# Attention output by way of DRAM, twenty output projections in the last attention stage, smaller loads of x and other idle products

## The reference

```python
x = x + 0.5 * ffn(layernorm(x))    # router over 8 experts, one chosen, gate = its probability
x = x + attn(layernorm(x))         # 16 heads of 8 features, rope, causal softmax, @ Wo.T
x = x + 0.5 * ffn(layernorm(x))    # the same weights again

# ffn, on t tokens
idx = argmax(softmax(xt @ Wr + br)); gates = max(...)
xn = layernorm(xt) * ln_g + ln_b
h = relu(xn @ W1[idx] + b1[idx]);  y = (h @ W2[idx] + b2[idx]) * gates
# attn
score = q @ k.T, masked above the diagonal
out = softmax(score / sqrt(8)) @ v;  return out @ Wo.T
```

## Time and profile before

| | us |
|---|---|
| median of three runs | 799.37 (796.62 to 800.66) |
| profiled execution | 801.17 |
| its span, first to last instruction | 799.4 |
| TensorE busy | 760.2 (95%), 5441 instructions |
| VectorE busy | 609.4 (76%) |
| ScalarE busy | 506.5 (63%) |
| GpSimd busy | 313.7 (39%) |
| mean granted clock of TensorE, share of full | 0.975 |

### The profile page before, as it was taken

One profiled execution on the slowest core, in us unless ns is written; L12 is line 12 of the kernel. 1 busy time (PEld: TensorE's weight loads), 2 busy tenths in 40 slices (PEclk: granted clock), 3 DMA queues, 4 the chain that ended last, 5 costly groups with the idle time before them and its releaser, 6 DMA issues. The chain is left out here.

```text
span 799.4 us, 17413 instructions
## 1 busy us (share of the span) xinstructions
PE 760.2 (95%) x5441; PEld 427.2 (53%) x5441; DVE 609.4 (76%) x1919; ACT 506.5 (63%) x1229; POOL 313.7 (39%) x603
## 2 busy tenths in 40 slices
PE   9989999898999999999999999999999988999994
PEld 6669897555433344333434444443344337578894
DVE  5557775489998988898889888988988706856663
ACT  2146663376357787778778777877787782066662
POOL 6067754156522234223322332242234220077753
PEclk8799999999999999999999999999999998999998
DMA  9712211227550332033113312330330001222210
GB/s 283 290 46 53 54 43 46 96 55 194 150 90 18 54 62 47 16 61 61 35 29 60 62 24 39 63 54 15 55 62 3 1 2 36 111 53 52 52 38 27
DMA packets 27990, 51.85 MB, mean 65 GB/s; under 512 B 7552, under 2 KB 19200, under 8 KB 26496
## 3 DMA queue, kind: packets, MB, share of 16 engines
q1 hardware_dynamic: 21296, 41.04, 22.0%
q0 software_dynamic: 4096, 8.69, 4.1%
q10 hardware_dynamic: 2512, 1.06, 0.5%
HBM read 35.40 MB, written 14.97 MB: 63 GB/s over the span
## 5 line engine op out<-in xcount | busy, mean ns | idle before, releaser
L1424 DVE CUSTOM_DVE_ANT_0 cst<-psS,mask_row 128x768 bf16<-128x768 f32 (+7 forms) x512 | 361.9, 755 | 41.8 <-PE psS L1297 37.8
L1387 ACT ACTIVATE prob<-psST 128x512 f32<-128x512 f32 (+3 forms) x750 | 320.2, 498 | 108.2 <-PE psST L1329 87.2
L1344 PE MATMUL a_psO<-prob,vs 128*32 128x512 f32 (+3 forms) x1536 | 157.5, 496 | 0.4 <-ACT p_anT L1393 0.2
L1495 POOL TENSOR_TENSOR a_gate<-a_zeros 1x1 f32<-1x1 f32 x128 | 23.4, 183 | 290.9 <-ACT prob L1387 290.7
L1329 PE MATMUL psST<-a_qs,ks 75*128 75x512 bf16 (+1 forms) x480 | 125.8, 328 | 0.0
L1297 PE MATMUL psS<-ks,a_qs 72*128 72x512 bf16 (+2 forms) x480 | 112.4, 326 | 0.1
L790 POOL DMA_INDIRECT tok<-rows,f_there_number x64 | 61.7, 963 | 89.4 <-DVE f_number L489 42.5
L1329 PEld LDWEIGHTS psST<-a_qs,ks 75*128 75x128 bf16 x480 | 42.7, 97 | 80.5 <-ACT prob L1387 50.4
L1496 POOL TENSOR_SCALAR_AFFINE_SELECT prob<-prob 128x512 f32<-128x512 f32 x128 | 79.9, 625 | 0.0
L1329 PE MATMUL psST<-qs,ks 75*128 75x512 bf16 (+3 forms) x270 | 71.8, 328 | 0.1
L1297 PE MATMUL psS<-ks,qs 72*128 72x512 bf16 (+3 forms) x288 | 67.8, 327 | 0.6 <-DVE a_rowmax L1424 0.3
(11 more groups left out here) (185 smaller groups left out, 1071.0 us busy)
## 6 DMA issues: line engine op xcount, KB each, us to landing
a_qs<-q_split SPq DMA_DIRECT2D x60, 96.0 KB
rows<-tok SPq DMA_DIRECT2D x8, 536.0 KB, 4.2
ks<-k_split SPq DMA_DIRECT2D x32, 128.0 KB
qs<-q_split SPq DMA_DIRECT2D x36, 96.0 KB
q_split<-p_part SPq DMA_DIRECT2D x24, 128.0 KB, 2.4
k_split<-p_part SPq DMA_DIRECT2D x24, 128.0 KB, 2.4
ks<-k_split SPq DMA_DIRECT2D x16, 192.0 KB
tok<-x_after_first SPq DMA_DIRECT2D x4, 536.0 KB, 5.3
```

The lines of the kernel that those rows point to most:

```text
L1344: last = nc.tensor.matmul(psO[32 * h:32 * h + 32, c0:c0 + w], vs[r][:, j, h, :], prob[:, u % RING, h, 0:w], start=(j == 0), stop=(u + 1 in ...
L1387: nc.scalar.activation(prob[:, u % RING, h, 0:w], score_buffer(s, u * QH + h)[:, 0:w], ACT.Exp, scale=SCALE).then_inc(exp_done, 1)
L1424: last = nc.vector.tensor_tensor_reduce(out=out[:, a * CH:a * CH + width], in0=ps[:, a * CH:a * CH + width], in1=mask_row[:, S - width:], ...
```

## The change

**Output by feature.** `copy_out` has two buffers `outT`. SP stores each half (`keep`, 128 x 512, with the sums among its rows) to DRAM (`o_dram`) and fetches the 32 rows of values into `shared`, which now lies by feature (`attended`). Once a batch the sums are fetched as 128 x 64, VectorE inverts them (`invert`), they are stored and fetched again, spread over the rows (`inverse`), and GpSimd multiplies (`divide`, two of 128 x 512). `A` and `B` are gone from `FIRST` and `MIDDLE`. Only the last stage's rows go the old way, transposed, divided and then turned back by four products (`turn_back`, letter `C`).

**Projections in the last stage.** Ten times `p`: two tiles of `shared` times `out_and_router`, and `add_project` on VectorE. The second feed-forward part projects only groups 5 to 7, without transposes or copies; five idle products stand before group 7.

**Others.** x comes in five portions of 4, 4, 8, 8 and 8 tiles. Idle products have new counts, `IDLE_LOGITS` 2 or 1 from the second group on. The order strings and `COPIES` are new, the scaling of the early logits moves from the end of `project` to the first `add_project`.

```diff
+LATE_TILES = 20
...
-IDLE_FIRST, IDLE_LOGITS, IDLE_CHOICE, IDLE_RANKS, IDLE_NUMBERS, IDLE_AMID, IDLE_ITEMS = 20, 1, (14, 47), 2, 17, 2, (7, 8)
+IDLE_FIRST, IDLE_LOGITS, IDLE_CHOICE, IDLE_RANKS, IDLE_NUMBERS, IDLE_AMID, IDLE_ITEMS = (
+    7, (1, 2), (14, 43), 2, 20, (3, 1, 1, 0), (7, 10))
+IDLE_LAST = 5
+
+PORTIONS = ((0, 4), (4, 8), (8, 16), (16, 24), (24, 32))
...
-    eng.dma_start(n.tok[:, b * TB:(b + 1) * TB, 0:D],
-                  n.x[b].rearrange("(n p) d -> p n d", p=P)).then_inc(n.x_loaded[b], 16)
+def load_x(eng, n, i):
+
+    first, last = PORTIONS[i]
+    eng.dma_start(n.tok[:, first:last, 0:D],
+                  n.x.rearrange("b (n p) d -> p (b n) d", p=P)[:, first:last, :]).then_inc(n.x_loaded[i], 16)
...
-                for t in range(NT):
+                for t in range(LATE_TILES if r == 1 else 0, NT):
                     g = t // CB
-                    if r == 0 and t % TB == 0:
-                        dve.wait_ge(n.x_loaded[t // TB], 16)
+                    if r == 0 and t == PORTIONS[portion(t)][0]:
+                        dve.wait_ge(n.x_loaded[portion(t)], 16)
                     if r == 1 and t % CB == 0:
-                        dve.wait_ge(multiplied, g + 1)
+                        dve.wait_ge(multiplied, g + 1 - LATE_TILES // CB)
                         for i in range(2):
                             there_, both = slice(t + 2 * i, t + 2 * i + 2), attended[g % 2][i]
-                            nc.vector.tensor_tensor(logit[:, there_, :], n.early[:, there_, :], both[:, :, D:], ALU.add)
+                            nc.vector.tensor_tensor(n.early[:, there_, :], n.early[:, there_, :], both[:, :, D:], ALU.add)
                             x = n.tok[:, there_, 0:D]
                             last_ = nc.vector.tensor_tensor(x, x, both[:, :, 0:D], ALU.add)
                         last_.then_inc(added, 1)
-                        dve.wait_ge(added, g + 1)
+                        dve.wait_ge(added, g + 1 - LATE_TILES // CB)
                     link.then(nc.vector.bn_stats(n.tok[:, t, D:], n.tok[:, t, 0:D]))
...
-            def turn(after, g):
-                u = turn_of[after, g]
-                wait(pe, turned_copied, u - 1)
+            def turn(g):
+                wait(pe, turned_copied, g - 1)
                 for j in range(CB):
-                    last = nc.tensor.transpose(wide_ps[u % 2][:, j * P:(j + 1) * P],
-                                               (n.shared if after else n.tok)[:, g * CB + j, 0:D], n.c("ident"))
+                    last = nc.tensor.transpose(wide_ps[g % 2][:, j * P:(j + 1) * P], n.tok[:, g * CB + j, 0:D],
+                                               n.c("ident"))
                 last.then_inc(turned, 1)
 
             def project(g):
-                u = turn_of[True, g]
-                pe.wait_ge(turned_copied, u + 1)
-                wait(pe, added, g - 1)
+                wait(pe, added, g - 1 - LATE_TILES // CB)
                 for j in range(CB):
-                    last = nc.tensor.matmul(attended[g % 2][j // 2][:, j % 2, :], xT[u % XT][:, j * P:(j + 1) * P],
+                    last = nc.tensor.matmul(attended[g % 2][j // 2][:, j % 2, :], n.shared[:, g * CB + j, :],
                                             n.out_and_router, start=True, stop=True)
                 last.then_inc(multiplied, 1)
 
             def router(g):
...
-                    pe.wait_ge(n.x_loaded[g // NCH], 16)
-                    turn(False, g)
+                    pe.wait_ge(n.x_loaded[portion(CB * g)], 16)
+                    turn(g)
                     if g == 1:
                         pe.wait_ge(n.router_centred, 1)
                     if g >= 1:
                         router(g - 1)
-                    if 2 <= g:
-                        idle(nc, n, psW, IDLE_LOGITS)
+                        idle(nc, n, psW, IDLE_LOGITS[g % 2])
...
-                turn(True, 0)
-                turn(True, 1)
-                for g in range(G):
+                for g in range(LATE_TILES // CB, G):
+                    if g == G - 1:
+                        idle(nc, n, psW, IDLE_LAST)
                     project(g)
-                    if g + 2 < G:
-                        turn(True, g + 2)
...
-                if t == TB - 1:
-                    idle(nc, n, psW, IDLE_AMID)
+                if t % TB == TB - 1:
+                    idle(nc, n, psW, IDLE_AMID[t // TB])
...
-    FIRST = ("offofoffoffoofoffffofffofffoffomfffofoffoffffofsfsofffsoffoffoffoffsossofsossffsoffstwtstssssNtt"
-             "wtwtsstsswsststwtstssststwstsstswtsstswMtssAsststswststsswssts")
-    MIDDLE = ("sstswtstsstswssNtstswstsstswwsstssBstsstwstsstsstwssttsswtssAsststwssMsttsswssttssswwsts")
-    LAST = ("ssswswssssNsswssssswssssswwssssssBssswssswsssswsssswsssswssssAwww")
-
-    COPIES = {FIRST: (5, None), MIDDLE: (6, 2), LAST: (6, 1)}
-    OWN_MASKS = 2
+
+    FIRST = ("oofffofofffoofofoffffffofoffoffmfffofoffofffofssosffofffsofffoffofsoffossfosfsfsofsftwtstssssNtt"
+             "wtwtssstswsststwststssststwtssstwtstssstwMsststsswststsswssts")
+    MIDDLE = ("sstswtstwssNsttswsststsswssstssstwstsstswtstssstwsststsswststssstwMssttsswsststsswwsts")
+    LAST = ("spsswwsssssNpspsspsswwssssspssswwsspsssspsswwssssAsswwsssCsspsspsswsssspwww")
+
+    COPIES = {FIRST: (5, None), MIDDLE: (6, 1), LAST: (6, 2)}
+
+
+    INVERT_AFTER, LAST_INVERT_AFTER = (12, 13), (6, 7)
+    OWN_MASKS = 1
...
+    def fetches(s):
+
+        found = [("rows", of, ch) for of, ch in ((s - 2, 1), (s - 1, 0)) if of >= 0]
+        if s == NST - 1:
+            found.append(("rows", s - 1, 1))
+        batch = s // QB - 1
+        if batch >= 0 and s % QB == 1:
+            found += [("weights", batch, ch) for ch in range(NCH)]
+        if batch >= 0 and s % QB == 2:
+            found += [("inverse", batch, ch) for ch in range(NCH)]
+        if s == NST - 1:
+            found += [("weights", B - 1, ch) for ch in range(NCH)]
+        return found
...
+        def keep(s, ch):
+
+            sp.wait_ge(out_copied, 2 * s + ch + 1)
+            sp.dma_start(n.o_dram[ch, s, :, :], outT[ch][:, :]).then_inc(kept, 16)
+
+        def fetch(what, of, ch):
+
+            if what == "rows":
+                sp.dma_start(attended[of % QB * RW:(of % QB + 1) * RW, ds(of // QB * S + ch * CH, CH)],
+                             n.o_dram[ch, of, :, :].rearrange("(h r) t -> h r t", h=QH)[:, 0:DK, :]).then_inc(fetched, 16)
...
         def stage(s):
             if s > 0:
                 load_max(s, s % RING, 1)
+            if s == NST - 1:
+                keep(s - 1, 1)
+            found = fetches(s)
+            if found:
+                sp.wait_ge(kept, 16 * (2 * s - (s < NST - 1)))
+                wait(sp, fetched, fetched_by(s - 1))
+            for what, of, ch in found:
+                if what == "weights":
+                    wait(sp, inverse_kept, 16 * NCH * of)
+                elif what == "inverse":
+                    sp.wait_ge(inverse_kept, 16 * NCH * (of + 1))
+                    wait(sp, divided, NCH * of)
+                fetch(what, of, ch)
+            if 0 < s < NST - 1:
+                keep(s - 1, 1)
             if s > 0 and s + 2 < NST:
                 load(s + 2, (s + 2) % RING)
+            if s < NST - 1:
+                keep(s, 0)
+            if s > QB and s % QB == 1:
+                keep_inverse(s // QB - 1)
             if s + 1 < NST:
                 load_max(s + 1, (s + 1) % RING, 0)
...
+        keep_inverse(B - 1)
+        sp.wait_ge(inverse_kept, 16 * NCH * B)
+        sp.wait_ge(divided, NCH * (B - 1))
+        sp.wait_ge(fetched, fetched_by(NST - 1))
+        for ch in range(NCH):
+            fetch("inverse", B - 1, ch)
...
+        def turn_back(ch, index, ps, normalised):
+
+            use(index)
+            pe.wait_ge(use_read, normalised + 1)
+            for b in range(CB):
+                last = nc.tensor.matmul(ps[P - RW:P, b * P:(b + 1) * P], divided_rows[ch][:, b, :], n.c("ident"),
+                                        start=True, stop=True)
...
+        def project(p, index, ps):
+
+            use(index)
+            pe.wait_ge(divided, 2 * p // CB + 1)
+            for j in range(2):
+                last = nc.tensor.matmul(ps[:, j * WIDE:(j + 1) * WIDE], n.shared[:, 2 * p + j, :], n.out_and_router,
+                                        start=True, stop=True)
...
-            wait(act, out_read, 2 * s + ch)
-            nc.scalar.activation(outT[:, :], psO[:, :], ACT.Copy).then_inc(out_copied, 1)
+            wait(act, kept, 16 * min(2 * s + ch, 2 * NST - 2))
+            nc.scalar.activation(outT[ch][:, :], psO[:, :], ACT.Copy).then_inc(out_copied, 1)
...
+        def add_project(p, index, ps):
+
+            tiles_, both = slice(2 * p, 2 * p + 2), ps[:, 0:2 * WIDE].rearrange("p (j c) -> p j c", c=WIDE)
+            if p == 0:
+                nc.vector.tensor_tensor(n.early[:, :, :], n.early[:, :, :],
```

(27 more changed lines are left out.)

114 lines of the change are left out of this document (78 added, 36 removed).

## The result

The changed kernel takes 795.3 us (median of 14 runs, 791.77 to 796.96), the kernel before, run beside it, 800.85 (14 runs, 796.18 to 802.34): a ratio of 0.9937, 95% interval 0.9921 to 0.9954. That is 5.6 us less, where 15.0 were forecast; 795.3 lies above the range (774 to 792). The profiled execution took 794.85 us, its span is 793.1.

The account below looks back on a forecast made before the run. TensorE was taken to bound the middle stages, VectorE the second feed-forward part's front, the clock the start; -12.3 - 0.4 + 2.7 + 1.8 - 9.4 + 0.6 + 2.0 = -15.0 us from 799.37 gave 784.4, range 774 to 792.

Parts of the forecast that it names:

- Tail: After the last division: last 32 rows turned back by four products, copied and signalled, +1.8 us (bounds +1.3, +4).
- Rival 4: Last stage: waits for sums, reciprocal, store and fetch put the whole chain behind the stage, +5 us, 789.5; chance 0.05.
- Middle stages: Fourteen attention stages: two groups of transposes go, 0.88 us of TensorE each stage, -12.3 us (bounds 6 and 20).
- rival 2: Middle stages set by TensorE's waits for exponentials, not its sum: half of the 12.3 us lost, 790.5; chance 0.08.
- First stage: First attention stage: loses one group of transposes, -0.4 us; its 48 idle products only change places.
- SP's queue and the transfers: Middle stages: added stores, fetches and waits on SP's queue stay hidden, with some 3 us to spare before delay costs.
- Last stage: Last attention stage: ten projections and the way back added, one transpose group and waits go, +2.7 us (bounds +1, +5).
- Front of the second part: Start of the second feed-forward part: three groups left of eight, 8.9 instead of 18.3 us, -9.4 us (bounds -8, -10.6).
- Ranking: Slot products, twice: three more idle products each, 1.3 us, about half where TensorE waits for VectorE, +0.6 us.
- Start: First 30 us: fewer front idle products, clock falls to half from 9 to 30 us, +2.0 us (bounds 0, +3.5).
- it falls at 8.7: Start: clock falls at 8.7 us, six groups take 3.0 us each, ending at 28.9 instead of 26.3, +2.6 us.
- Rival 1: Start: the clock holds at full, 7.2 us less than forecast, 777.2; chance 0.28.

Follow-up runs that it names:

- the late instruction: Kernel before, plus one one-element GpSimd instruction that waits for VectorE's last division; executed once, span 800.3 us, next block +2.87 us after the last copy.
- without the round trip: Changed kernel without the way through DRAM (no stores, fetches, reciprocals or divisions by it; most attended rows zero): 792.34 us, ratio 0.9874.
- the last kernel: Changed kernel with 20 front idle products, VectorE dividing behind its last projection, both reciprocals behind projection 6, 18 idle products before the first item: 780.43 us, ratio 0.9746.

## Why the prediction was wrong, point by point

- **Tail, +1.8 (bounds 1.3 to 4), measured +6.12.** The step that failed is the reading of the pause of 3 us in the earlier trace rows as following VectorE's division; it followed GpSimd's last mask. I had the second chain (store, fetch, two multiplications on GpSimd) end "about where the other does", and it did, 1.4 us later; but an end on GpSimd is followed by 5.8 us and one on VectorE by 0.5. Shown by two kernels that moved the ends: with GpSimd's taken out of the way the block came 5.41 us sooner, with one put late it came 2.87 us later. The row that would have told stood in the trace of before: GpSimd idle after 656.55, the block 5.61 us later. Rival 4 had the place and nearly the price (+5), with the wrong reason.
- **Middle stages, -12.3 (bounds -6 to -20), measured 14 x 0.66 = -9.2** (the -9.42 of the table has the first stage too, and one disturbed period of 27.07 us). Inside the bounds, but the step "TensorE sets the middle stages, so 0.88 us go one to one" was wrong: that work was worth 0.08 us in the old order. The 103 waits of the earlier trace rows, which I took for products still running because none is longer than 0.8 us, were the hint, and rival 2 was nearer for the old order. That 0.66 came out all the same, inside the bounds, is luck: it took the new order, which I had costed at nothing, together with the missing transposes.
- **First stage, -0.4.** Measured -0.8 from its first-half copy to the next; in the old order without transposes it was 0.14. Which part of its new order gave the rest wasn't tried.
- **SP's queue and the transfers, hidden.** Right: the period is the same without them.
- **Last stage, +2.7, measured +2.65.** Right, by its steps: start to start the projections take 4.93 us (forecast 4.6) and the products of the way back 0.99 (0.9), and scores and weighings together take 2.8 us less than before (2.3).
- **Front of the second part, -9.4, measured -9.40 (18.25 to 8.85).** Right, by its steps: VectorE's first step comes 2.19 us after the block's first product (2.1), and the third group starts 1.2 us late (1).
- **Ranking, +0.6 for both.** Measured up to the slot numbers +0.68 in the first and +0.66 in the second, twice the 0.3 each. But by the first score of stage 0 only +0.17 of it are left, and by the end +0.20 of the second: the idle products delay the numbers, and most of the delay is taken up behind them.
- **Start, +2.0 (bounds 0 to 3.5), measured +3.37.** The direction was right, and the reason half: I let the clock fall where before it fell too, but with 7 products it wasn't up for the first groups. The third group's transposes began at 10.06 instead of the 9 us of the sum; from there to the last router products, at 28.14, it took 18.08 us, as the sum had it (18, with the 1.5 idle products). So even the +2.6 of the case "it falls at 8.7" was too small, and I had taken +2.0 as a mean with a later fall. Six kernels have this start: in five traces the clock was half from the first product to 32 us or later, in one (the kernel with the divisions on VectorE) it was full from 4.63 to 8.05 and half again until 31.94, with the choice at 28.72. Rival 1, that the clock holds in the kernel as changed, didn't come; its price was right for 20 products at the front (choice at 20.6 to 21.7 in five kernels). And the 26.62 of before, from which I counted, is one of two outcomes of that start.

## What to carry to other kernels

Before a serial stretch between blocks is costed, look at which engine ended last and how long the pause is behind each: work that must come last belongs on the engine with the short one, here VectorE and not GpSimd. An engine busy in 40.00 of 40 us isn't thereby the bound; take its work away in the trace's own order first, and take the order of letters as a change of its own, for here each alone was worth nothing or less. Idle products for the clock are to be set by the state they leave (full or half), read from more than one trace, and ended before the data they wait for.

## What the hardware showed that I had not expected

- From GpSimd's last instruction to the first product of the next block: 5.61, 5.59, 5.78, 5.61, 5.78 and 5.61 us (before; with the late instruction; changed; without the round trip; with 20 idle products; the last kernel). The longer value came each time behind the two multiplications. Behind VectorE it was 0.54, in both kernels in which it divides last.
- One start, two outcomes: the same instructions gave a choice at 26.62 to 27.22 us in three traces and at 19.61 to 20.71 in three. And a choice 3.4 us sooner can end in a slower kernel than the changed one (798.92 against 795.3), by a fall of the clock 180 us later.
